# Gated slot attention with a SwiGLU block: q projection and output product change places, and some VectorE and queue work is moved with them

## The reference

```python
x = x + attention(layernorm(x))          # Wq, Wk, Wv, Wg, Ws, Wo; 16 heads, 64 key, 128 value features, 64 slots
x = x + ffn(layernorm(x))                # gate/up/down weights rounded to fp8, width 1536
# attention, per head:
s = clip(x @ Ws, -32, 32);  z = cumlogsumexp(s);  p = exp(s - z);  g = exp(z_prev - z)
hk = hk * g + k_t * p_t;    ok = q_t . hk
pv = softmax(ok)
hv = hv * g + p_t * v_t;    ov = pv . hv
o = ov * rsqrt(mean(ov**2) + eps) * g_norm * silu(x @ Wg);   y += o @ Wo
```

## Time and profile before

| | |
|---|---|
| median of 3 runs | 1405.77 us (1404.84 to 1406.28) |
| profiled execution | 1406.31 us, of which 1404.6 us span |
| granted TensorE clock | 0.999 of full speed |
| TensorE busy | 1349.2 us, 96% |
| VectorE, ScalarE, GpSimd busy | 1056.7, 424.8, 138.5 us |
| chain that ended last | TensorE 80%, VectorE 13%, SyncE's queue 3% |

### The profile page before, as it was taken

One profiled execution on the slowest core, in us unless ns is written; L12 is line 12 of the kernel. 1 busy time (PEld: TensorE's weight loads), 2 busy tenths in 40 slices (PEclk: granted clock), 3 DMA queues, 4 the chain that ended last, 5 costly groups with the idle time before them and its releaser, 6 DMA issues.

```text
span 1404.6 us, 23184 instructions
## 1 busy us (share of the span) xinstructions
PE 1349.2 (96%) x8819; PEld 1122.9 (80%) x8819; DVE 1056.7 (75%) x1681; ACT 424.8 (30%) x1214; POOL 138.5 (10%) x106
## 2 busy tenths in 40 slices
PE   6999999999999999999999999999999999999997
PEld 5787788778777877887788778877888878888886
DVE  8788877888788888888888888878778875535454
ACT  4333323332332233223322332333233333222221
POOL 3001101110111012001200120012010010000000
PEclk9999999999999999999999999999999999999999
DMA  5255445444544455446444544454331530000000
GB/s 180 53 126 122 98 93 133 115 98 91 136 105 98 92 140 115 98 91 146 95 106 107 132 95 105 117 123 96 70 98 41 154 121 1 31 0 30 0 30 31
DMA packets 429274, 130.34 MB, mean 93 GB/s; under 512 B 302192, under 2 KB 420336, under 8 KB 429168
## 3 DMA queue, kind: packets, MB, share of 16 engines
q1 hardware_dynamic: 429168, 128.91, 38.7%
HBM read 78.72 MB, written 50.14 MB: 92 GB/s over the span
## 4 chain that ended last, share of the span: by engine, by line
PE 80%; DVE 13%; SPq 3%; issue 2%; DMA 1%; ACT 1%; POOL 0%; DVEq 0%; ACTq 0%
PE bank L463 16%; PE bank L465 15%; PE bank L464 15%; PE bank L117 12%; PE bank L1593 6%; PE bank L682 4%; DVE o L1136 3%; DVE oT_lo L1022 3%; DVE o L1119 2%; PE bank L665 2%; PE bank L595 2%; PE bank L523 2%; PE bank L670 1%; SPq L324 1%; SPq L359 1%
## 5 line engine op out<-in xcount | busy, mean ns | idle before, releaser
L463 PE MATMUL bank<-wvg_hi,xT_hi 128*128 128x512 f32 x512 | 205.8, 402 | 0.6 <-POOL wvg_lo L965 0.6
L465 PE MATMUL bank<-wvg_hi,xT_lo 128*128 128x512 f32 x512 | 199.7, 390 | 0.0
L464 PE MATMUL bank<-wvg_lo,xT_hi 128*128 128x512 f32 x512 | 199.7, 390 | 0.0
L1054 DVE SCALAR_TENSOR_TENSOR g<-tanh_half_g,bank 128x256 f32<-128x256 f32 x128 | 52.6, 411 | 107.4 <-ACT tanh_half_g L792 107.4
L463 PE MATMUL bank<-wo_hi,oT_hi 128*128 128x512 f32 x256 | 102.4, 400 | 27.4 <-DVE oT_lo L1022 27.4
L742 ACT ACTIVATE a_and_v<-bank 128x256 f32<-128x256 f32 x128 | 48.9, 382 | 243.4 <-PE bank L465 243.4
L463 PEld LDWEIGHTS bank<-wvg_hi,xT_hi 128*128 128x128 f32 x512 | 96.2, 188 | 23.3 <-issue 1.8
L465 PEld LDWEIGHTS bank<-wvg_hi,xT_lo 128*128 128x128 f32 x512 | 96.1, 188 | 20.3
L464 PEld LDWEIGHTS bank<-wvg_lo,xT_hi 128*128 128x128 f32 x512 | 96.3, 188 | 17.9
L1046 DVE RECIPROCAL cT<-cT 128x512 f32<-128x512 f32 x32 | 107.3, 3353 | 1.1
L994 POOL TENSOR_TENSOR rstd<-ssq,neg_half 128x8 f32<-128x8 f32 x32 | 52.4, 1637 | 552.3 <-DVE ssq L1101 552.3
(11 more groups left out here) (164 smaller groups left out, 3034.9 us busy)
## 6 DMA issues: line engine op xcount, KB each, us to landing
o_transposed<-o SPq DMA_DIRECT2D x27, 512.0 KB, 3.2
oT_lo<-o_transposed SPq DMA_DIRECT2D x108, 128.0 KB, 3.0
fp_weights<-q SPq DMA_DIRECT2D x28, 318.0 KB, 2.7
e_tokens<-k_tok_then_wT SPq DMA_DIRECT2D x31, 256.0 KB, 2.3
e_tok<-e_tokens SPq DMA_DIRECT2D x124, 64.0 KB, 2.4
c_tokens<-cT SPq DMA_DIRECT2D x31, 256.0 KB, 2.4
cT<-c_tokens SPq DMA_DIRECT2D x124, 64.0 KB, 2.3
k_tokens<-p SPq DMA_DIRECT2D x31, 192.0 KB, 2.9
```

Of the source, the lines that this page charges most:

```text
L463: pe.matmul(dst, w_hi, m_hi, start=(k == 0), stop=False)
L464: pe.matmul(dst, w_hi, m_lo, start=False, stop=False)
L465: last = pe.matmul(dst, w_lo, m_hi, start=False, stop=(k == n - 1))
L1054: dve.scalar_tensor_tensor(out=g[i % 2][:, c, :, :].rearrange("p a d -> p (a d)"), in0=th[:, :], scalar=1.0, in1=job_bank(VGS[c], i)[:, 2 ...
```

## The change

TensorE: QT goes directly behind ok, and the output product behind QT. In units 0 and 1, which have no output product, VG0 takes its place ahead of the weights' transposes. ScalarE: the copy of the queries comes ahead of the copy of the transposed weights (`wT_evac`), and the second split of an output weight (`split_o(.., 1)`) goes behind VG1's evacuation. VectorE: `o_turn` and `lo_vg` go behind the softmax. SyncE: `store_o` goes behind `load_e`, `load_oT` behind `store_k`, and `load_vg` to the end of the round.

```diff
@@ block.sync
             load_q8(u)
-            if u - 1 <= FAR:
-                store_o(u - 1)
             if i == 2:
                 load_skq(pair, 1)
             store_e(u + 1)
-            if i == 1:
-                load_vg(pair)
             load_e(u + 1)
             if u - 1 <= FAR:
-                load_oT(u - 1)
+                store_o(u - 1)
             store_k(u + 1)
...
+            if u - 1 <= FAR:
+                load_oT(u - 1)
             store_c(u + 1)
             load_k(u + 1)
             load_c(u + 1)
             if i == 1:
                 load_skq(pair, 0)
+                load_vg(pair)
             store_q8(u)
@@ block.tensor
             v = product_of(u)
+            if not last:
+                job(QT, nu, ni)
             if v is None:
-                job(QT, nu, ni)
+                job(VG0, nu, ni)
             else:
...
             w_transposes(u)
             if v is not None and not last:
-                job(QT, nu, ni)
+                job(VG0, nu, ni)
             if not last:
-                job(VG0, nu, ni)
                 job(VG1, nu, ni)
@@ block.scalar
-            if product_of(u) is not None:
+            if last:
                 wT_evac(u)
-            if last:
                 ffn.fuse_hi(act, 0, 0)
                 ffn.tanh(act, 0, 1)
             if not last:
                 evac(QT, nu, ni)
-            if product_of(u) is None:
+            if product_of(u) is not None and not last:
                 wT_evac(u)
...
             if not last:
                 evac(VG0, nu, ni)
+            if product_of(u) is None:
+                wT_evac(u)
+            if not last:
+                evac(VG1, nu, ni)
             if outputs:
                 split_o(u // B, 1)
-            if not last:
-                evac(VG1, nu, ni)
@@ block.vector
             value_states(u)
-            if u and u - 1 <= FAR:
-                o_turn(u - 1)
             if u > FAR + 1:
                 out_lo(u - 1, A)
             elif u > 1:
                 far_lo(u - 2)
-            if i == 3 and not tail:
-                for k in range(2):
-                    lo_vg(pair_of_next(u), k)
...
                                      op0=ALU.mult, op1=ALU.mult).then_inc(s_es, 1)
+            if u and u - 1 <= FAR:
+                o_turn(u - 1)
+            if i == 3 and not tail:
+                for k in range(2):
+                    lo_vg(pair_of_next(u), k)
```

## The result

| | before | after |
|---|---|---|
| median | 1406.03 us (4 runs) | 1373.21 us (1372.34 to 1373.75, 4 runs) |
| ratio | | 0.9767, 95% interval 0.9751 to 0.9784 |
| profiled execution, span | 1406.31, 1404.6 us | 1373.29, 1371.6 us |
| granted TensorE clock | 0.999 | 0.998 |

The kernel is 32.8 us faster, against 34 forecast (1373.2 us against 1372.0). In the changed kernel the lines of what follows have shifted a little: the product's matmuls are L462 to L464, the subtractions L1023, gates L1055.

The account below looks back on a forecast made before the run. TensorE, busy 96%, was taken as the bound, so only its idle time could move: 33.6 + 1.3 + 2.2 - 3.3 = 33.8 us off the profiled 1406.3 gave 1372.5, as median 1372.0 us; range 1366 to 1381.

Parts of the forecast that it names:

- The wait and its price: Output product's wait for the turned heads' low part, units 2 to 27: 27.4 us plus 0.24 each, 33.6 us gained.
- the weighted values': Three waits in units with i = 1, caused by ScalarE's second output-weight split holding VG1's evacuation: 2.2 us gained.
- Cover: With QT ahead, the product starts at +3.44 us behind ok, after the subtraction at +2.46 at worst: all 26 waits go.
- The delays don't add: Units with i = 1, 2, 4: later product hides VectorE's turn; gate 0 ends at +15.9, 1.5 us slack, no cost.
- Rival (2): Product's and turn's delays add, gate 0 moves 3.4 us to +18.0 in 19 units, more in seven: 1390 us; chance 0.07.
- Units with i = 3: VectorE's and GpSimd's subtractions alternate, VectorE's ending at +1.0; gate 0 at about +17.0, no cost taken, bound 7 us.
- Rival (1): Units with i = 3 wait at VG2 by the subtractions' old length, 7 x 1.0 us more: 1379 us; chance 0.14.
- The tail: Units 29 and 30: additions and statistics make gate 0 late for VG2, 1.65 us lost twice, 3.3 us; bounds 0 to 4.
- Units 0 and 1: VG0 ahead of the weights' transposes, VG2 held by gate 0: 1.3 us gained, between 0 and 3.8.
- the row of VG2 behind `g`: Sign in TensorE's waits: VG2 waiting for gate 0, 3 to 4 us in units 29, 30, 0 and 1.
- The queue: SyncE's reordered stores and loads cost nothing; the loads of c_tok would be late first, with some 10 us.
- Rival (3): Add_y-to-gate-0 chain slips each unit; gain gone at 2.75 us, 1418 us at 3.2: slower than before; chance 0.04.

Follow-up runs that it names:

- turn_alone: Kernel before the change plus VectorE's and SyncE's part alone, TensorE and ScalarE in their old order: 1379.39 us.
- qt_alone: Kernel before the change plus TensorE's and ScalarE's part alone, VectorE and SyncE in their old order: 1372.87 us.
- pool_late: turn_alone with GpSimd's half of the value weights' rest (units with i = 3) held until the softmax is done: 1381.53 us.
- Both remedies: Changed kernel with units 29 and 30 in the old TensorE and ScalarE order, 1370.13 us; or with their statistics behind gate 0, 1370.14 us.
- old_queue: Changed kernel with all of SyncE's old order: 1376.52 us.
- extra4: Changed kernel with four unused reductions (2.87 us) on VectorE between the additions to y and the turn of the keys, every unit but the last: 1436.12 us.
- extra2: Changed kernel with two unused reductions (1.43 us) on VectorE between the additions to y and the turn of the keys, every unit but the last: 1389.39 us.

## Why the prediction was right

- **The wait and its price.** 33.6 + 2.2 us were forecast for units 2 to 27, 35.6 came. That this is so close is in part luck: the product's wait was worth 33.0, since up to 0.04 us a unit of the "wait plus 0.24 us" does not last until the next ST, and the weighted values' was worth 2.6. The two misses cancel. The cause given for the 2.2 us, ScalarE's split, is one of two (see turn_alone).
- **Cover.** That the product's wait goes even with the old lateness of the subtractions (+2.46 against +3.44) was the step that carried the most; qt_alone shows it by itself: the whole gain with VectorE's old order.
- **The delays don't add.** Gate 0's end was forecast at +15.9 for i = 1 and measured at +15.79 in unit 17 (621.63 - 605.84). Rival (2) is out.
- **Units with i = 3.** The forecast order, VectorE's first subtraction, GpSimd's, VectorE's second, gave +1.0 and +17.0; measured +0.98 and +16.90, and the single rows of unit 19 (last section) show this order, with GpSimd's first ending at +0.44 for +0.45. pool_late shows that GpSimd is the cause of the length. Rival (1) is out.
- **The tail.** 3.3 us lost were forecast, with VG2 at +19.2 from ok; it came at 1028.47 - 1009.39 = +19.08. Both remedies give 3.0 us back. The whole stretch lost 3.5 us; 0.5 of it lies behind the start of ok in unit 31, and its cause is open.
- **Units 0 and 1.** 1.1 us gained for 1.3, and VG2 does wait for gate 0. One sign was too small: the row of VG2 behind `g` was to hold 3 to 4 us and holds 5.5, because 2.6 us of units 0 and 1 are in it beside the 2.9 of units 29 and 30. The gain there was forecast by places in time, not by this row, so the sum does not change.
- **The queue.** "I cost it at nothing" is right for the change as it is. The slack I had counted, some 10 us for the loads of c_tok, was not that of the tightest item: in the old order old_queue shows that to be the load of the second output weight half, because ScalarE holds an evacuation behind it.
- **The point where it turns.** Here a size was wrong, which the forecast didn't need. Rival (3) put the point from which the gain is gone at 2.75 us of additional lateness, with 1.5 us of slack in all 27 units. But units with i = 3 have 0.5 us and units 0, 1, 29 and 30 none; with these, 20 x (L - 1.6) + 7 x (L - 0.5) + 4 x L = 33 gives an estimate of 2.2 us for the same point. Measured: 1.43 us cost 16 us, 2.87 us cost 63 us, 30 more than the gain. The waits made 48.5 of the 63; the clock, which I had not reckoned with, made the rest.

## What to carry to other kernels

When one engine is busy 96% and waits once a round for a chain on another, put a piece of its own work that depends on nothing in that chain ahead of the waiting one, and compare its length with the longest wait, not with the mean. Then follow what the moved piece delays: here everything behind the output product, of which the next item with a consumer (gate 0 for VG2) had 1.5 us, 0.5 us or, in units 0, 1, 29 and 30, less than nothing. Two remedies for the same wait don't add (33 and 27 us gave 33); price each on what the other leaves. Here the part of TensorE and ScalarE alone (qt_alone) gives all of it; the late turn adds nothing and needs the queue's new order to cost nothing.

## What the runs showed of the hardware that I had not expected

A TensorE wait can cost more than its length. Behind waits of 2.2 to 4.2 us on an otherwise busy engine the granted clock was at its lower level for part of the next microseconds (0.50 from 313 to 314, 0.71 over 312.2 to 318.0). It cost 1.1 to 2.3 us each (up to L683) in eight of eleven such units of extra4 and three of the four longest waits of extra2. In the kernel before, with waits of up to 1.8 us in the attention units, the clock never fell there. The Trainium skill (TensorE: Matmul & The Clock Gate, Part 1: The HAM clock gate) tells of two clock levels and of a fall after idle time; the trace agrees on the levels, 1.00 and 0.50, and on a fall behind idle time. Why three units with the same wait of 2.2 us were spared, no run here shows.

Two subtractions on VectorE and two on GpSimd that start 0.33 us apart interleave one by one. Unit 19 of the changed kernel, each instruction by itself:

```profile
670.42 0.68 DVE L1023 TENSOR_TENSOR oT_lo<-oT_lo,oT_hi 128x512 fp32r<-128x512 f32 x1
670.75 1.50 POOL L966 TENSOR_TENSOR wvg_lo<-stage_vg,wvg_hi 128x512 fp32r<-128x512 f32 x1 [5.22 <-ACT wvg_hi L742]
671.02 1.77 DVE L1023 TENSOR_TENSOR oT_lo<-oT_lo,oT_hi 128x512 fp32r<-128x512 f32 x1
672.21 1.75 POOL L966 TENSOR_TENSOR wvg_lo<-stage_vg,wvg_hi 128x512 fp32r<-128x512 f32 x1
```

The first on VectorE takes its usual 0.68 us; the ends then come in turn, GpSimd 672.25, VectorE 672.79, GpSimd 673.96. VectorE's pair takes 2.37 us instead of 1.28, GpSimd's 3.21 us. The step behind them on VectorE, which reads PSUM and one SBUF tile, takes its usual 0.68 us (672.72 to 673.40) while GpSimd is at work until 673.96.
